# A transformer layer's tail in another order: one projection in the last attention step, a norm ahead of a gate, other work between products of one bank

## The chip, the cores and the metric

The kernel runs on one core of one Trainium2 chip. The metric is device microseconds (us) for one execution; a profile of one execution is read beside it. Engines: PE is TensorE (PEld are its weight loads), DVE is VectorE, ACT is ScalarE, POOL is GpSimd, SP is the engine that issues most transfers. PE writes its results into PSUM, which has eight banks, 0 to 7; DVE and ACT read them from there.

## The reference

```python
x = x + cross_attention(layernorm(x), ctx, ctx, mask)   # 16 heads of 16, 4096 keys, scores masked
x = x + retention(layernorm(x))                         # 4 heads, keys of 64, values of 128, rotary, decay, gated
x = x + experts(layernorm(x))                           # 8 dense experts, softmax gate, threshold 0.1

# retention(x): q, k, v, g = x Wq', x Wk', x Wv', x Wg';  q, k rotated
o = (q k' * decay) v;  o = o * rsqrt(mean(o * o) + eps) * gnorm_w
return (o * g * sigmoid(g)) Wo'
# experts(x): w = softmax(x Wgate + b); w[w < 0.1] = 0; w = w / sum(w)
return sum_e w[:, e] * (x W_e + b_e)
```

There are 2 batches of 256 queries with 256 features, so 512 rows of x: four tiles of 128 rows, t = 0 to 3. Tiles 0 and 1 are the first batch, tiles 2 and 3 the second.

## The kernel before, in words

Almost everything is float32 in SBUF, and every engine's program is one list written out by hand. Engines meet only through counting semaphores: `wait_ge(s, n)` holds an engine, and all that stands behind in its list, until the counter has reached n.

**The attention steps.** `steps` runs 56 steps (NU), seven blocks of 128 keys for each of eight stages (a stage is four heads of one batch). In step n PE computes the scores of step n (`scores`, L811) into banks 4 and 5, ACT takes their exponentials (`exps`, L1269), and PE multiplies those of step n-1 with the values (`weighted`, L826) into bank 6. Scores of the next step wait until ACT has read the bank. When a stage is complete, ACT copies the sums out (`outputs_out`, L1257), PE turns them into bank 7 (`turn_outputs`, L793), and DVE copies them into `acc` (`combine`, L1632). The last stage's copy, turn and combine stand at the very end of `steps`.

**Work of the first batch inside the steps.** The first batch's attention is complete long before step 46 (AT_TURNED). In step 46 PE turns its two tiles (`turn_at` 0 and 1, L878), in step 47 ACT takes them (`take_at`), in step 49 PE multiplies with the output weights (`attention_out` 0 and 1, L898), and in step 50 DVE, after `combine` of stage 6, adds the residual (`first_stream(0)`, L1663, needs `o_ready`) and computes the norm ahead of the retention (`layernorms`, L1485 to L1480). A norm is a chain of some dozen small DVE instructions in which each waits for the one before, and it ends with two wide ones (L1480) that write `xn`.

**The tail.** `tail_of_all` holds the rest. DVE first divides the second batch's attention by its sums (`attention_tokens(1)`, L1656), which needs the last `combine`. PE turns the normed tiles 0 and 1 (`turn_xn`), and per tile computes three projections of 512 columns each (`project_ret(t, m)`, L917): m = 0 is q and k into bank 2, m = 1 is v into bank 3, m = 2 is the gate into bank 4. Between those of tile 0 stand `turn_at(2)`, `turn_at(3)` and `attention_out` of 2 and 3. Each bank is single: `project_ret(t, m)` for t over 0 waits until the reader of tile t-1 is done, for bank 4 that is DVE's `gate_product` (L1697, needs ACT's tanh, L1320, and counts `gated_ready`). DVE's list for t = 0: the rotary products of bank 2 (L1678 to L1693), `first_stream(1)`, `gate_product(0)`, and then the second batch's norm.

Turned tiles go through banks 0 and 1, later bank 0 alone, in the fixed order TURNS; a turn waits for ACT's take of the turn before it (`turn_taken`). Outputs of the retention, gate logits and biases (SIDES) share bank 2 in the same manner: each waits until DVE has read the one before (`side_taken`).

Then follow, on PE: retention scores and values of the first batch, the last projections, and for the outputs `retention_out(t)` (L990, eight instructions into bank 2), read by DVE at L1736. The experts come in pairs: `pair(t, pr)` (L1010) multiplies a tile with two experts' weights in two halves over the input features (c = 0 and 1, weights in `ctxT` and `kpart`), into one of four banks (5, 6, 1, 7 in turn), and waits until DVE has read what stood there four pairs ago (`pair_read`). DVE adds each expert with its weight (`add_experts`, L1773), which needs the gate weights; those are computed for two tiles at a time (`gate_weights`, L1759 to L1765, last one writes `nwts`) and turned by PE (`turn_weights`) for the bias product (`biases`, L1021). Each tile is written out when its eight experts have been added.

Of the kernel before, what the change touches and what calls it, by code (L numbers as in the profile page):

```python
# [202 lines left out]
def build(nc, a):  # L203
    with ExitStack() as ctx:
# [437 lines left out]
        def _(pe):  # L642
# [188 lines left out]
            def steps(c):  # L831
                for n in range(NU):
# [29 lines left out]
                    if n == AT_TURNED + 3 and not c.loop:  # L862
                        attention_out(0)
                        attention_out(1)
                weighted(c, NU - 1)
                turn_outputs(c, STAGES - 1)
# [42 lines left out]

            def tail_of_all():  # L910
                def project_ret(t, m):

                    taken("n2", t)
                    if t:
                        pe.wait_ge(s[("rope_read", "v_taken", "gated_ready")[m]], t)
                    for c in range(KIN):
                        mm = pe.matmul(bank[:, 2 + m, :], xnT[:, c, t * P:(t + 1) * P], w_ret[:, c, m * 512:(m + 1) * 512],  # L917
                                       start=(c == 0), stop=(c == KIN - 1))
                    mm.then_inc(s["proj_ready"], 1)

# [4 lines left out]
                pe.wait_ge(s["late_loaded"], 16 * 10)  # L925
                turn_xn("n2", 0)
                turn_xn("n2", 1)
                for t in range(TT - 1):
                    project_ret(t, 0)
                    if t == 0:  # L930
                        turn_at(2)
                        turn_at(3)
                    if t:
                        turn_qk(t - 1)
                    project_ret(t, 1)
                    if t == 0:
                        attention_out(2)
                        attention_out(3)
                    if t:
                        turn_xn("n2", t + 1)  # L940
                    project_ret(t, 2)
# [62 lines left out]
                def pair(t, pr):  # L1004

                    m = t * (NE // 2) + pr
                    if m >= len(PAIR_BANKS):
                        pe.wait_ge(s["pair_read"], 2 * (m - len(PAIR_BANKS) + 1))
                    for c in range(KIN):
                        mm = pe.matmul(bank[:, PAIR_BANKS[m % 4], :], xnT[:, c, t * P:(t + 1) * P],  # L1010
                                       w_exp[c][:, 2 * pr:2 * pr + 2, :], start=(c == 0), stop=(c == KIN - 1))
                    mm.then_inc(s["pair_ready"], 1)
# [13 lines left out]
                retention_out(0)  # L1026
                retention_out(1)

                ret_values(RH)
# [17 lines left out]
                retention_out(2)  # L1047
                retention_out(3)
                turn_weights(1)
                pair(1, 0)  # L1050
# [9 lines left out]
                pair(2, 1)  # L1060
                turn_weights(2)
                pair(2, 2)
# [68 lines left out]
            with pe.If(fast < 1):  # L1131
# [25 lines left out]
                attention_out(1)  # L1157
                tail_of_all()

        @block.scalar  # L1160
        def _(act):
# [109 lines left out]
            def steps(c):  # L1271
                for n in range(NU):
# [11 lines left out]
                    if n == AT_TURNED + 1 and not c.loop:  # L1284
                        act.wait_ge(s["wo_loaded"], 32)
                        take_at(0)
                        take_at(1)
                outputs_out(c, STAGES - 1)
# [21 lines left out]
            def tail_of_all():  # L1310
# [33 lines left out]
                take_xn("n2", 0)  # L1344
                take_xn("n2", 1)
# [73 lines left out]
            with act.If(fast < 1):  # L1419
# [17 lines left out]
                take_at(1)  # L1437
                tail_of_all()
# [3 lines left out]
        def _(dve):  # L1442
# [191 lines left out]
            def steps(c):  # L1634
                for n in range(NU):
# [7 lines left out]
                    if n == AT_TURNED + 4 and not c.loop:  # L1643
# [23 lines left out]
            def tail_of_all():  # L1667
# [31 lines left out]
                for t in range(TT - 1):  # L1699
# [4 lines left out]
                    if t == 0:  # L1704
                        first_stream(1)
                    gate_product(t)
                    if t == 0:
                        layernorms("dve_post", x1, range(QT, TT), "n2_ready")
# [176 lines left out]
```

## Time and profile before

| what | value |
|---|---|
| median of three runs | 241.67 us |
| lowest, highest of them | 239.74, 241.96 us |
| the profiled execution's own time | 239.15 us |
| its span, first to last instruction | 237.2 us |
| PE, DVE, ACT busy, share of the span | 91%, 65%, 47% |
| mean granted TensorE clock | 0.995 |

Times in rows are us from the span's start. A row of the timeline gives start, duration, engine, line, operation, result <- operands, and in brackets how long the engine stood idle before and which instruction ended that. Ends of matmuls are modelled, and the next one can start a little before the row's end. "x4" merges four instructions that follow each other. A float32 matmul appears as two instructions.

### The profile page before, as it was taken

How to read it: one execution, taken by the hardware profiler on the slowest of the kernel's cores; microseconds unless marked ns; L12 is line 12 of the kernel's file. 1: busy time of each engine (PE TensorE's matmuls, PEld its weight loads, DVE VectorE, ACT ScalarE, POOL GpSimd, SP SyncE). 2: the span in 40 equal slices, each digit the busy share in tenths (PEclk: the TensorE clock that was granted, in tenths of full speed). 3: DMA queues.
4: the chain of work that ended last, by engine and by line, in shares of the span. 5: the costliest groups of instructions: out<-in, count | busy, mean ns of one | idle time of the engine just before them, and what ended most of it. 6: DMA issues, size and time to landing. Idle time of an engine off the chain costs nothing.

```text
span 237.2 us, 3690 instructions
## 1 busy us (share of the span) xinstructions
PE 215.2 (91%) x1314; PEld 115.7 (49%) x1314; DVE 154.4 (65%) x352; ACT 111.5 (47%) x238; POOL 36.6 (15%) x45
## 2 busy tenths in 40 slices
PE   8799997889799999999998989988988998899892
PEld 8367543344454544444443535445746754544340
DVE  6793888954928479787880346585184728585682
ACT  3227855575557487878889664233242051101000
POOL 8006998204503100000000000000000000000000
PEclk9999999999999999999999999999999999999998
DMA  5699673777099000920000000000000000000000
GB/s 182 216 228 322 191 199 94 190 185 260 14 237 221 4 1 3 284 73 3 3 3 1 0 3 1 0 0 0 3 0 0 0 4 1 0 0 22 23 26 26
DMA packets 15391, 17.93 MB, mean 76 GB/s; under 512 B 2600, under 2 KB 14472, under 8 KB 15368
## 3 DMA queue, kind: packets, MB, share of 16 engines
q1 hardware_dynamic: 14072, 17.30, 25.9%
q10 hardware_dynamic: 1296, 0.34, 0.8%
q8 instruction: 12, 0.20, 0.4%
q14 instruction: 11, 0.09, 0.1%
HBM read 9.79 MB, written 0.52 MB: 43 GB/s over the span
## 4 chain that ended last, share of the span: by engine, by line
PE 60%; DVE 16%; DMA 6%; ACT 5%; POOL 5%; issue 4%; SPq 3%; POOLq 0%; DVEq 0%; ACTq 0%
PE bank L826 10%; PE bank L811 10%; PE bank L1010 8%; PE bank L751 7%; PE bank L917 6%; DVE cneg L1592 4%; PE bank L990 3%; PE bank L878 3%; PE bank L711 3%; DMA ctxT<-in_ctxT 3%; DMA mask_all<-in_mask 2%; ACT prob L1269 2%; PE bank L698 2%; SPq L400 2%; PE bank L898 2%
## 5 line engine op out<-in xcount | busy, mean ns | idle before, releaser
L1592 DVE TENSOR_REDUCE cneg<-bank 128x1 f32<-128x896 f32 x64 | 68.1, 1087 | 24.2 <-PE bank L751 23.4
L1269 ACT ACTIVATE prob<-bank 128x512 f32<-128x512 f32 x112 | 65.6, 597 | 24.2 <-PE bank L811 21.7
L811 PE MATMUL bank<-qstack,kstack 100*128 100x256 bf16 x224 | 42.3, 274 | 3.4 <-ACT prob L1269 2.0
L751 PE MATMUL bank<-kstack,qstack 97*128 97x448 bf16 x128 | 34.7, 353 | 3.1 <-DVE cneg L1592 3.0
L826 PE MATMUL bank<-prob,vals 128*32 128x256 f32 x448 | 35.8, 391 | 0.4 <-ACT prob L1269 0.4
L811 PEld LDWEIGHTS bank<-qstack,kstack 100*128 100x128 bf16 x224 | 17.3, 97 | 31.6 <-ACT prob L1269 15.6
L917 PE MATMUL bank<-w_late,xnT 128*128 128x512 f32 x48 | 22.0, 595 | 0.3 <-ACT xnT L1298 0.3
L1010 PE MATMUL bank<-ctxT,xnT 128*128 128x512 f32 x32 | 17.1, 616 | 0.3 <-DVE x_in L1773 0.3
L1773 DVE SCALAR_TENSOR_TENSOR x_in<-bank,nwts,x_in 128x256 f32<-128x256 f32 x32 | 15.5, 484 | 2.5 <-PE bank L1010 1.4
L1010 PE MATMUL bank<-kpart,xnT 128*128 128x512 f32 x32 | 16.3, 592 | 0.0
L751 PEld LDWEIGHTS bank<-kstack,qstack 97*128 97x128 bf16 x128 | 11.5, 98 | 8.9 <-DVE cneg L1592 4.2
L826 PEld LDWEIGHTS bank<-prob,vals 128*32 128x32 f32 x448 | 8.8, 108 | 14.3 <-issue 11.2
L698 PE MATMUL bank<-ctxT,wk 128*128 128x448 f32 x32 | 13.3, 548 | 0.4 <-DMA ctxT<-in_ctxT 0.3
L711 PE MATMUL bank<-wv,ctxT 128*128 128x256 f32 x56 | 13.0, 381 | 0.1
L1632 DVE COPY acc<-bank 128x136 f32<-128x136 f32 x8 | 2.4, 299 | 15.7 <-PE bank L793 15.5
L917 PEld LDWEIGHTS bank<-w_late,xnT 128*128 128x128 f32 x48 | 8.5, 190 | 8.2 <-issue 7.7
L1298 ACT ACTIVATE xnT<-bank 128x256 f32<-128x256 f32 x8 | 3.0, 383 | 19.7 <-PE bank L878 19.7
L711 PEld LDWEIGHTS bank<-wv,ctxT 128*128 128x128 f32 x56 | 10.4, 190 | 2.1 <-DVE cneg L1592 0.4
L1010 PEld LDWEIGHTS bank<-kpart,xnT 128*128 128x128 f32 x32 | 6.1, 190 | 7.6 <-issue 7.6
L990 PE MATMUL bank<-w_late,kstack 128*128 128x256 f32 x32 | 7.7, 384 | 1.3 <-DVE mask_all L1736 1.3
L698 PEld LDWEIGHTS bank<-ctxT,wk 128*128 128x128 f32 x32 | 5.8, 190 | 5.3 <-issue 4.1
L1232 ACT COPY vals<-bank 128x512 f32<-128x512 f32 (+3 forms) x6 | 3.9, 658 | 8.7 <-PE bank L711 8.7
(151 smaller groups left out, 260.2 us busy)
## 6 DMA issues: line engine op xcount, KB each, us to landing
kstack<-kpart SPq DMA_DIRECT2D x24, 224.0 KB
w_late<-in_w_ret SPq DMA_DIRECT2D x1, 1536.0 KB
mask_all<-in_mask SPq DMA_DIRECT2D x2, 512.0 KB, 5.1
ctxT<-in_w_exp SPq DMA_DIRECT2D x1, 1024.0 KB
kpart<-in_w_exp SPq DMA_DIRECT2D x1, 1024.0 KB
ctxT<-in_ctxT SPq DMA_DIRECT2D x2, 448.0 KB, 5.5
ctxT<-in_ctxT SPq DMA_DIRECT2D x1, 896.0 KB, 7.4
qstack<-acc SPq DMA_DIRECT2D x12, 64.0 KB, 3.0
```

The costliest lines, as they stand in the source:

```text
L698: mm = pe.matmul(bank[:, c.key_banks(n) + h, 0:HC], wk[:, i, f * P:(f + 1) * P], ctxT[:, b, i, h * HC:(h + 1) * HC], start=(i == 0), stop= ...
L711: mm = pe.matmul(out[:, (k - blocks[0]) * D:(k - blocks[0] + 1) * D], ctxT[:, b, i, k * P:(k + 1) * P], wv[:, i, :], start=(i == 0), stop= ...
L751: mm = pe.matmul(out, qstack[0:MROW + 1, h, b, qt * P:(qt + 1) * P], kstack[0:MROW + 1, b, h, half_ * HC:(half_ + 1) * HC], start=True, st ...
L811: mm = pe.matmul(out[:, hh * NQ:(hh + 1) * NQ], kstack[0:KROWS, b, h, kt * P:(kt + 1) * P], qstack[0:KROWS, h, b, :], start=(hh == 0 or no ...
L826: mm = pe.matmul(bank[32 * j:32 * j + PADV, OB, 0:NQ], vals[:, b, kt, e:e + PADV], prob[:, (2 * u + j // 2) % PROBS, (j % 2) * NQ:(j % 2 + ...
L878: mm = pe.transpose(out[:, f * P:(f + 1) * P], src[:, f * width:(f + 1) * width], ident[:, :])
L917: mm = pe.matmul(bank[:, 2 + m, :], xnT[:, c, t * P:(t + 1) * P], w_ret[:, c, m * 512:(m + 1) * 512], start=(c == 0), stop=(c == KIN - 1))
L990: mm = pe.matmul(out[:, 0:D], yT[:, c, t * P:(t + 1) * P], w_reto[:, c, :], start=(c == 0), stop=(c == 3))
L1010: mm = pe.matmul(bank[:, PAIR_BANKS[m % 4], :], xnT[:, c, t * P:(t + 1) * P], w_exp[c][:, 2 * pr:2 * pr + 2, :], start=(c == 0), stop=(c = ...
L1269: act.activation(prob[:, n % PROBS, :], bank[:, S0 + jj, :], ACT.Exp).then_inc(c["prob_ready"], 1)
L1592: dve.tensor_reduce(cneg[:, st % 2, i:i + 1], bank[:, pair:pair + 2, 0:HC], AXXY, ALU.max, negate=True).then_inc(c["max_read"], 1)
L1773: dve.scalar_tensor_tensor(x_in[:, t, :], src, nwts[:, t, e:e + 1], x_in[:, t, :], ALU.mult, ALU.add).then_inc(s["pair_read"], 1)
```

## The change

It touches the order of instructions only; what is computed, and every buffer and bank, stays.

1. In the steps, `attention_out` of tiles 0 and 1 moves from step 49 to 48; DVE's `first_stream(0)` and the first batch's norm move from step 50 to 48, and so ahead of `combine` of stage 6.
2. The turns of the normed tiles 0 and 1 and ACT's takes of them move from the start of the tail to the end of the steps, ahead of the last `weighted` (PE) and ahead of the last `outputs_out` (ACT). `project_ret(0, 0)` moves ahead of the last `turn_outputs`.
3. DVE computes the second batch's norm before `gate_product(0)` and not after it.
4. `ret_values(RH)` moves between `retention_out(0)` and `retention_out(1)`.
5. `pair(1, 0)` is split: its first half goes between `retention_out(2)` and `retention_out(3)`, its second behind `turn_weights(1)` as before.
6. `pair(2, 2)` moves ahead of `turn_weights(2)`, so the two turns of weights stand next to each other.

```diff
@@ PE, steps
-                    if n == AT_TURNED + 3 and not c.loop:
+                    if n == AT_TURNED + 2 and not c.loop:
                         attention_out(0)
                         attention_out(1)
+                if not c.loop:
+                    turn_first_half()
                 weighted(c, NU - 1)
+                if not c.loop:
+                    project_ret(0, 0)
                 turn_outputs(c, STAGES - 1)
@@ PE, new function
+            def turn_first_half():
+
+                pe.wait_ge(s["late_loaded"], 16 * 10)
+                turn_xn("n2", 0)
+                turn_xn("n2", 1)
@@ PE, tail_of_all
-                pe.wait_ge(s["late_loaded"], 16 * 10)
-                turn_xn("n2", 0)
-                turn_xn("n2", 1)
                 for t in range(TT - 1):
-                    project_ret(t, 0)
+                    if t:
+                        project_ret(t, 0)
                     if t == 0:
                         turn_at(2)
                         turn_at(3)
...
-                def pair(t, pr):
+                def pair(t, pr, halves=(0, 1)):
 
                     m = t * (NE // 2) + pr
-                    if m >= len(PAIR_BANKS):
+                    if m >= len(PAIR_BANKS) and 0 in halves:
                         pe.wait_ge(s["pair_read"], 2 * (m - len(PAIR_BANKS) + 1))
-                    for c in range(KIN):
+                    for c in halves:
...
                 retention_out(0)
+                ret_values(RH)
                 retention_out(1)
 
-                ret_values(RH)
...
                 retention_out(2)
+                pair(1, 0, (0,))
                 retention_out(3)
                 turn_weights(1)
-                pair(1, 0)
+                pair(1, 0, (1,))
                 biases(1)
...
                 pair(2, 1)
+                pair(2, 2)
                 turn_weights(2)
-                pair(2, 2)
                 turn_weights(3)
                 biases(2)
@@ ACT, steps and tail_of_all
+                if not c.loop:
+                    take_xn("n2", 0)
+                    take_xn("n2", 1)
                 outputs_out(c, STAGES - 1)
...
-                take_xn("n2", 0)
-                take_xn("n2", 1)
@@ DVE, steps
-                    if n == AT_TURNED + 4 and not c.loop:
+                    if n == AT_TURNED + 2 and not c.loop:
                         first_stream(0)
                         layernorms("dve_post", x1, range(QT), "n2_ready")
@@ DVE, tail_of_all
                     if t == 0:
                         first_stream(1)
+                        layernorms("dve_post", x1, range(QT, TT), "n2_ready")
                     gate_product(t)
-                    if t == 0:
-                        layernorms("dve_post", x1, range(QT, TT), "n2_ready")
```

The branch for a mask that the fast path can't handle gets the same calls in the same order; it isn't taken with these inputs. Line numbers in the changed kernel are higher by 4 (L878 to L882, L898 to L902), 3 (L917 to L920), 8 (L990 to L998, L1010 to L1018), 10 (L1021 to L1031) and 16 (DVE's).

How instructions stand on PE at the end of the steps, before. L811 are scores, L826 `weighted`, L793 the last `turn_outputs`, L878 turns (of `xn`, the normed tiles, and of `vals`, the second batch's attention), L917 projections:

```order
L811 MATMUL bank<-qstack,kstack 128x256 x4
L826 MATMUL bank<-prob,vals 32x256 x8
L793 MATMUL bank<-ident,outT 128x128 x2
L878 MATMUL bank<-ident,xn 128x128 x4
L917 MATMUL bank<-w_late,xnT 128x512 x2
L878 MATMUL bank<-ident,vals 128x128 x4
L917 MATMUL bank<-w_late,xnT 128x512 x2
```

The same place on PE after the change:

```order
L811 MATMUL bank<-qstack,kstack 128x256 x4
L826 MATMUL bank<-prob,vals 32x256 x4
L882 MATMUL bank<-ident,xn 128x128 x4
L826 MATMUL bank<-prob,vals 32x256 x4
L920 MATMUL bank<-w_late,xnT 128x512 x2
L793 MATMUL bank<-ident,outT 128x128 x2
L882 MATMUL bank<-ident,vals 128x128 x4
L920 MATMUL bank<-w_late,xnT 128x512 x2
```

The four turns of `xn` have moved between the last two `weighted`, and the first projection has moved from behind the turn of `outT` to ahead of it; the turns of `vals` now follow that turn directly.

On DVE, in the tail for tile 0, before: L1690 and L1693 end the rotary work, L1663 is `first_stream(1)`, L1697 `gate_product(0)`, and from L1485 on it is the second batch's norm, of which the start is shown:

```order
L1690 TENSOR_TENSOR kstack<-kstack 128x8x32
L1693 TENSOR_TENSOR kstack<-kstack 128x8x32
L1663 TENSOR_TENSOR mask_all<-bank,xbo 128x256 x2
L1697 SCALAR_TENSOR_TENSOR kstack<-kstack,bank 128x512
L1485 BN_STATS stats<-mask_all 128x6 x2
L1473 BN_AGGR moments<-stats 128x2 x2
```

And on DVE after the change, the end of the same norm and what follows it (L1496 is the norm's last line, L1713 `gate_product`, L1694 to L1709 the rotary work of tile 1):

```order
L1482 TENSOR_TENSOR nw<-nw 128x2
L1483 SCALAR_TENSOR_TENSOR nw<-nw 128x2
L1496 TENSOR_SCALAR xn<-mask_all,moments,nw 128x256 x2
L1713 SCALAR_TENSOR_TENSOR kstack<-kstack,bank 128x512
L1694 TENSOR_TENSOR kstack<-bank,rope 128x512
L1695 TENSOR_TENSOR kstack<-bank,rope 128x512
```

The gate product now comes after the whole norm and right before the rotary products of tile 1.

On PE among the experts of tile 2, before: L1010 in twos is one pair, L878 of `nwts` a turn of gate weights, L1021 the bias product:

```order
L1010 MATMUL bank<-ctxT,xnT 128x512
L1010 MATMUL bank<-kpart,xnT 128x512
L878 MATMUL bank<-ident,nwts 8x128
L1010 MATMUL bank<-ctxT,xnT 128x512
L1010 MATMUL bank<-kpart,xnT 128x512
L878 MATMUL bank<-ident,nwts 8x128
L1021 MATMUL bank<-b_exp,wT 128x256
```

After:

```order
L1018 MATMUL bank<-ctxT,xnT 128x512
L1018 MATMUL bank<-kpart,xnT 128x512
L1018 MATMUL bank<-ctxT,xnT 128x512
L1018 MATMUL bank<-kpart,xnT 128x512
L882 MATMUL bank<-ident,nwts 8x128 x2
L1031 MATMUL bank<-b_exp,wT 128x256
```

Pair (2, 2) stands ahead of both turns of weights, and nothing stands between the two.

## Rows read from the trace of the kernel before

**Rows 1.** The page: busy us, share of the span, instructions of each engine.

```profile
PE 215.2 (91%) x1314; PEld 115.7 (49%) x1314; DVE 154.4 (65%) x352; ACT 111.5 (47%) x238; POOL 36.6 (15%) x45
```

**Rows 2.** Waits of PE: who <- for whom: us in total, times, longest.

```profile
PE bank L990 <- DVE mask_all L1736: 1.3, 2, 0.7
PE bank L878 <- DVE xn L1480: 1.2, 1, 1.2
```

**Rows 3.** Timeline of steps 47 to 50.

```profile
128.30 0.64 PE L826 MATMUL bank<-prob,vals 128*32 128x256 f32 x8
128.55 0.40 ACT L1298 ACTIVATE xnT<-bank,bv 128x128 f32<-128x128 f32 x1
...
130.87 2.00 PE L898 MATMUL bank<-wo,xnT 128*128 128x256 f32 x8
...
133.12 1.08 ACT L1269 ACTIVATE prob<-bank 128x512 f32<-128x512 f32 x2 [1.74 <-PE bank L811]
...
134.49 0.74 DVE L1663 TENSOR_TENSOR mask_all<-bank,xbo 128x256 f32<-128x256 f32 x2
```

**Rows 4.** Timeline of the last step and the start of the tail.

```profile
140.56 0.64 PE L826 MATMUL bank<-prob,vals 128*32 128x256 f32 x8 [0.39 <-ACT prob L1269]
141.26 0.37 ACT L1257 COPY outT<-bank 128x256 f32<-128x256 f32 x1 [0.76 <-PE bank L826]
141.69 0.44 PE L793 MATMUL bank<-ident,outT 128*128 128x128 f32 x2 [0.49 <-ACT outT L1257]
...
142.23 0.30 DVE L1632 COPY acc<-bank 128x136 f32<-128x136 f32 x1 [2.98 <-PE bank L793]
142.38 0.66 ACT L1298 ACTIVATE xnT<-bank 128x256 f32<-128x256 f32 x2 [0.74 <-PE bank L878]
...
142.81 1.98 PE L917 MATMUL bank<-w_late,xnT 128*128 128x512 f32 x4 [0.25 <-ACT xnT L1298]
142.95 0.76 DVE L1656 TENSOR_TENSOR vals<-acc,rsum 128x256 f32<-128x256 f32 x2
...
145.07 1.88 PE L917 MATMUL bank<-w_late,xnT 128*128 128x512 f32 x4
...
146.79 1.89 PE L898 MATMUL bank<-wo,xnT 128*128 128x256 f32 x8
```

**Rows 5.** Timeline of the second batch's residual, gate product and norm.

```profile
148.72 0.42 DVE L1663 TENSOR_TENSOR mask_all<-bank,xbo 128x256 f32<-128x256 f32 x1 [0.34 <-PE bank L898]
...
151.13 0.69 DVE L1697 SCALAR_TENSOR_TENSOR kstack<-kstack,bank 128x512 f32<-128x512 f32 x1 [1.99 <-ACT kstack L1320]
...
152.39 1.88 PE L917 MATMUL bank<-w_late,xnT 128*128 128x512 f32 x4
...
154.97 0.74 DVE L1480 TENSOR_SCALAR xn<-mask_all,moments,nw 128x256 f32<-128x256 f32 x2
155.44 0.44 PE L878 MATMUL bank<-ident,xn 128*128 128x128 f32 x2 [1.17 <-DVE xn L1480]
```

**Rows 6.** Timeline around the last gate weights.

```profile
217.77 1.00 DVE L1773 SCALAR_TENSOR_TENSOR x_in<-bank,nwts,x_in 128x256 f32<-128x256 f32 x2
...
220.25 0.27 PE L878 MATMUL bank<-ident,nwts 128*8 128x128 f32 x1 [0.99 <-DVE nwts L1765]
...
220.56 0.27 ACT L1298 ACTIVATE wT<-bank 8x128 f32<-8x128 f32 x1 [2.00 <-PE bank L878]
...
222.28 0.69 PE L1021 MATMUL bank<-b_exp,wT 8*128 8x256 f32 x2
```

**Rows 7.** Timeline: what PE waits for behind the two retention outputs.

```profile
188.30 0.56 DVE L1714 TENSOR_TENSOR kstack<-bank,decay 128x384 f32<-128x384 f32 x1
...
212.73 1.13 PE L1010 MATMUL bank<-ctxT,xnT 128*128 128x512 f32 x2 [0.31 <-DVE x_in L1773]
```

**Rows 8.** Stretches: length, PE, PEld, DVE, ACT, POOL busy; clock; DMA share, GB/s.

```profile
60.00:65.00 5.00, 3.59 (x31) 2.18 (x28) 4.73 (x6) 2.71 (x5) 2.50 (x2) 1.00 0.02 5
...
230.00:237.00 7.00, 2.58 (x7) 0.79 (x5) 2.19 (x5) 0.00 (x0) 0.00 (x0) 0.86 0.08 23
```

More of the change, by code:

```diff
@@ L907, in turn_xn, with project_ret @@
                 turn(kind, t, bank[:, turn_bank(kind, t), :], xn[:, t, :], KIN)
-            def tail_of_all():
[L911 to L915, printed above, removed]
-                    for c in range(KIN):
-                        mm = pe.matmul(bank[:, 2 + m, :], xnT[:, c, t * P:(t + 1) * P], w_ret[:, c, m * 512:(m + 1) * 512],
-                                       start=(c == 0), stop=(c == KIN - 1))
-                    mm.then_inc(s["proj_ready"], 1)
+            def project_ret(t, m):
+                taken("n2", t)
+                if t:
+                    pe.wait_ge(s[("rope_read", "v_taken", "gated_ready")[m]], t)
+                for c in range(KIN):
+                    mm = pe.matmul(bank[:, 2 + m, :], xnT[:, c, t * P:(t + 1) * P], w_ret[:, c, m * 512:(m + 1) * 512],
+                                   start=(c == 0), stop=(c == KIN - 1))
+                mm.then_inc(s["proj_ready"], 1)
+            def turn_first_half():
+                pe.wait_ge(s["late_loaded"], 16 * 10)
+                turn_xn("n2", 0)
+                turn_xn("n2", 1)
+            def tail_of_all():
                 def turn_qk(t):
@@ L923, in turn_qk @@
                     turn("qk", t, bank[:, TB, :], qk_rot[:, t % 2, :], 4)
-                pe.wait_ge(s["late_loaded"], 16 * 10)
-                turn_xn("n2", 0)
-                turn_xn("n2", 1)
                 for t in range(TT - 1):
-                    project_ret(t, 0)
+                    if t:
+                        project_ret(t, 0)
                     if t == 0:
@@ L1002, in logits @@
                     mm.then_inc(s["side_ready"], 1)
-                def pair(t, pr):
+                def pair(t, pr, halves=(0, 1)):
                     m = t * (NE // 2) + pr
-                    if m >= len(PAIR_BANKS):
+                    if m >= len(PAIR_BANKS) and 0 in halves:
                         pe.wait_ge(s["pair_read"], 2 * (m - len(PAIR_BANKS) + 1))
-                    for c in range(KIN):
+                    for c in halves:
                         mm = pe.matmul(bank[:, PAIR_BANKS[m % 4], :], xnT[:, c, t * P:(t + 1) * P],
-                                       w_exp[c][:, 2 * pr:2 * pr + 2, :], start=(c == 0), stop=(c == KIN - 1))
-                    mm.then_inc(s["pair_ready"], 1)
+                                       w_exp[c][:, 2 * pr:2 * pr + 2, :], start=(c == 0), stop=(c == KIN - 1),
+                                       skip_group_check=True)
+                    if KIN - 1 in halves:
+                        mm.then_inc(s["pair_ready"], 1)
                 def turn_weights(t):
@@ L1157, in _ @@
                 attention_out(1)
+                turn_first_half()
+                project_ret(0, 0)
                 tail_of_all()
@@ L1437, in _ @@
                 take_at(1)
+                take_xn("n2", 0)
+                take_xn("n2", 1)
                 tail_of_all()
```

## The prediction

> **What bounds the kernel now.** I read the page first. PE is busy for 91% of the span, DVE for 65% [rows 1], so what the order of the work can win is PE's idle time, and only where PE's own list is what ends last. Then I read PE's waits in the tail, after 138 us. Three are 1 us or more in total: for the reader of bank 2 between retention outputs (1.3 us in two waits) and for DVE's norm result `xn` (1.2 us, one wait) [rows 2], and for the last gate weights `nwts` (0.99 us, one wait) [rows 6]. Each edit from number 3 on aims at one of them. Last came the timeline, to see what ends each wait and what else stands in the way once it is gone.
>
> The steps are a loop between PE (scores) and ACT (exponentials); a PE instruction that has nothing to do with it lengthens a step when ACT runs dry. In step 49 that happens: `attention_out` holds PE for 2.00 us from 130.87, and ACT stands idle for 1.74 us before its next exponentials at 133.12 [rows 3].
>
> **Edits 1: output product and first norm in step 48.** Before, PE has issued `weighted` of step 47 at 128.30 and could go on at about 128.9; ACT's take of tile 1 ends at 128.55 + 0.40 = 128.95 [rows 3]. So `attention_out` (two times some 0.95 us) now runs from 128.9 to 130.8, in time in which PE partly waited for ACT. The two exponentials of step 49 follow: scores out at 130.8, and from PE's scores to ACT's start I take 0.4 us, so ACT begins at 131.2, needs 1.08 us for two [rows 3] and 0.37 for the copy of stage 6 [rows 4], and can start step 50 at about 132.7 instead of 133.12. That is 0.4 us won. The bounds: nothing, if the product only moves the wait by one step; 0.6 us if no part of it shows up again. I take 0.4. DVE starts the residual at about 130 and the norm at 131.4 rather than at 135.2; a norm takes 155.71 - 151.82 = 3.9 us [rows 5], so it is done at 135.4. `combine` of stage 6 waits behind it until 135.4; its bank 7 is next wanted by the last `turn_outputs` after 141 us [rows 4], six us later, so this costs nothing.
>
> **Edits 2: turns, takes and one projection in the last step.** All times here are those of before less the 0.4. The four turns of `xn` (0.43 us) fill PE's 0.39 us idle ahead of the last `weighted` [rows 4], so that stays at 140.15. ACT takes the two tiles in 0.66 us [rows 4], 140.1 to 140.8, and is free when the last `weighted` ends at 140.8: no cost to the copy of `outT`. PE then starts `project_ret(0, 0)` at 140.7, not 142.81 [rows 4]. Four instructions of 512 columns keep PE for 1.72 us (145.07 to 146.79, with nothing between [rows 4]), to 142.4. But the last `turn_outputs` stood at 141.69 and now stands behind them, at 142.4. What hangs on it: DVE's `combine` 0.54 us later, the reciprocal, and the two halves of the second batch's attention, done at about 143.37 and 143.71 before [rows 4], that is 1.7 and 2.0 us behind the turn. Now they are done at 144.1 and 144.45. PE's next instructions are exactly the turns of these tiles, so PE stands idle from 142.7 to 144.15: a wait of about 1.4 us that was not there. `project_ret(0, 1)` starts at about 144.75 against 145.07 [rows 4]. So the pair of edits 1 and 2 is worth 0.3 us, of which the first gave 0.4: moving the projection trades a filled gap for a new one and loses 0.1. Its bounds: had the turn not been delayed, 145.07 - 143.8 = 1.3 us would be won; were another 0.5 us lost on the way from `combine`, 0.4 is lost in place of 0.1.
>
> **Edit 3: the norm before the gate product.** Before, DVE has the residual at 149.14, stands idle for 1.99 us for tanh, does the gate product (151.13, 0.69 us), then the norm; `xn` of tile 2 arrives at 155.38 and PE starts its turn at 155.44 after 1.17 us idle [rows 5]. PE's queue was in fact free 1.72 us after 152.39, at 154.11, so the wait costs 1.33 us. After, the norm runs from 149.15 to 153.1 and the gate product to 153.8 (in times of before; both shift by the 0.3). `xn` is there at 152.8, ahead of PE at 154.1: the wait is gone. What is late next: `project_ret(1, 2)` writes bank 4 and so needs the gate product; PE gets to it at 154.4, 0.6 us after it is done. The rotary products of tile 1, queued behind the norm on DVE before as well, start at 153.9 instead of 155.75. So nothing follows that takes the gain back, and all 1.33 us pass through. Bounds: 1.17 (the row's idle time) and 1.33; I take 1.3.
>
> **Edits 4 and 5: nothing.** `ret_values(RH)` is three products of 128 columns, six instructions, some 0.65 us at the projections' 1.72 us for four times 512, and fills one of the two waits of [rows 2] (0.6 us). But the second `retention_out` can't start earlier, since it waits for DVE in either order. From its result DVE runs residual, norm and, inside the norm, two decay products; PE's last retention values wait for the one at 188.30 to 188.86 [rows 7], and the turn of `xn` after them for the end of the norm. The chain is DVE's, PE only waits later: 0. In the same way half of `pair(1, 0)` (0.86 us, half of four times 512 columns) fits into the other wait (0.7 us, plus the 0.16 by which a modelled end overlaps the next start, 145.07 + 1.88 - 146.79 [rows 4]), and PE has 0.86 us less to do behind; but pair (1, 3) waits at 212.73 for an expert that DVE adds inside and behind the third norm [rows 7], and the norm starts when `retention_out(3)` has ended. 0 again. Bounds for the two together: 0.2 us lost, where the filler is longer than the gap, and 1.1 us won, if PE and not DVE were last in both places; the rows say DVE, so I take 0.
>
> **Edit 6: pair (2, 2) ahead of both turns of weights.** Before, PE waits 0.99 us for `nwts` and turns at 220.25 [rows 6]; with the 0.16 its queue is free from 219.1. Pair (2, 2) needs the bank that expert 5 of tile 1 leaves at 218.77 [rows 6], before PE is there: no new wait. It fills 219.1 to 220.8, by when the weights (220.19) are there. Then come two turns in a row, and the second must wait for ACT's take of the first: 220.56 + 0.27 - 220.25 = 0.58 us after its start [rows 6] plus some 0.1 to come back, where nothing was waited for before and the turn itself took 0.2. So 0.5 us go back and 0.6 are won. From there PE has work without a gap to its end (biases, 0.69 us, then five pairs of 1.72 us), and DVE's last two experts follow the last pair: the gain reaches the end. Bounds: 0.3 if the take comes later, 1.1 if it costs nothing; I take 0.6.
>
> **Sum.** 0.4 - 0.1 + 1.3 + 0 + 0.6 = 2.2 us. Against the profiled execution: 239.15 - 2.2 = 236.95 us. The median of the runs is 241.67, 2.5 us above it, and the runs spread over 2.2 us; the time I forecast is 241.67 - 2.2 = 239.5 us, 0.9% below.
>
> **Rivals.**
> Rival A, the tail waits give more. If PE's list ends last at the places of edits 4 and 5, they add up to 1.1 us: 3.3 us, 238.4. For it: the waits of 1.3 us are real [rows 2]. Against: what follows them waits for DVE [rows 7].
> Rival B, a wait takes the place of another. The new 1.4 us wait for the attention tiles is longer (its chain is combine, reciprocal, product, turn over two engines), and edit 6's second turn waits for more than its 0.5: then edit 3 alone stays, 1.3 us, 240.4. For it: in both places the change itself makes the waiting instruction come sooner behind what it needs. Against: each link has its row.
> Rival C, the clock. The new idle stretch of PE before the turns, right behind the idle in the steps, lets the granted TensorE clock fall from 2.4 to 1.2 GHz, and the projections that follow run at half speed. Each us of PE's work at half clock costs one us; past 2.2 us of it the change is slower than before, and if it lasts for the 5 us of work from 144.2 on, the sum is -2.2 + 5 = +2.8: 244.5. For it: the granted clock did fall once, to 0.86 over the stretch from 230 to 237 us, after PE's last matmul had ended [rows 8]. Against: in 60 to 65 us PE was idle for 1.4 of 5 us and the clock stayed at 1.00 [rows 8].
> The Trainium skill ("TensorE: Matmul & The Clock Gate", Part 1) states that the gate halves the clock of an array that has been idle and gives it back only after sustained work. By that rule a reordering that gathers PE's idle time in one place can lose more than it moves; the stretch at 60 us does not show it for idle time of this size.
>
> **Chances.** Forecast (1.8 to 2.6 us won) 0.55; A or anything above 2.6 us 0.17; B 0.20; C 0.05; others 0.03. A measurement of this kernel tells about 1%, 2.4 us, from no change, and the forecast of 0.9% lies just inside, so its share is split by the noise: 0.29 faster, 0.26 within. With A's 0.17 that makes faster by over 1% 0.46; B, the rest and half of the others give within 1% 0.48; slower by over 1% is C and a rest, 0.06. The range: down to A and a low draw of the runs (the profiled 239.15 less 2.2 is 236.95) 236.8; up to B with the upper run of the spread, 241.3.
>
> **What would show it right or wrong.** In the profile of the changed kernel: ACT's idle time before step 50's exponentials falls from 1.74 us, and they start 0.4 us earlier; PE has a wait of about 1.4 us for the turns of the attention tiles; PE's 1.17 us wait for `xn` is gone and the first turn of tile 2 comes 1.6 us earlier than 155.44; the wait for bank 2 in front of `retention_out` is gone, but the distance from that output to the third norm and to pair (1, 3) is the same; between the two last turns of weights lie 0.6 us in which PE waits for ACT, and the bias product comes 2.2 us earlier than 222.28. Wrong it would be if the granted clock shows anything below 1.00 after 142 us, if `project_ret(1, 2)` waits for the gate product, or if the span from 156 us to the end shrinks by more than edit 6's 0.6 us.

## The result, and the profile after

The changed kernel takes 237.39 us (median of 4 runs, 237.17 to 239.12) against 240.83 (4 runs, 239.74 to 241.96): ratio 0.9887, 95% interval 0.9842 to 0.9932. Timed again later in 12 runs it gave 0.9914 (0.9875 to 0.9952). The forecast was 2.2 us, 0.9% less; the two measurements say 1.1% and 0.9%. In microseconds the forecast was 239.5. The profiled execution took 237.40 us with a span of 235.5, against 239.15 and 237.2.

The page's first rows of the changed kernel (busy us, share of the span, instructions), to be held against [rows 1]:

```profile
PE 215.2 (91%) x1314; PEld 115.7 (49%) x1314; DVE 154.5 (66%) x352; ACT 111.4 (47%) x238; POOL 36.7 (16%) x45
```

The work is the same to 0.1 us on each engine; only idle time went. PE's waits in the whole span of the changed kernel (who <- for whom: us, times, longest), against [rows 2]:

```profile
PE bank L977 <- DVE kstack L1729: 1.6, 2, 0.9
...
PE bank L882 <- DVE vals L1672: 1.2, 1, 1.2
...
PE bank L1018 <- DVE x_in L1788: 0.7, 2, 0.4
...
PE bank L882 <- ACT wT L1314: 0.4, 1, 0.4
```

All three waits the edits aimed at are gone from the list (bank 2's reader 1.3 us, `xn` 1.2, `nwts` 1.0). Four have grown or appeared: 1.2 us for the second batch's attention tiles (L882 <- L1672), which is edit 2's; the wait for the decay products (L977, from 1.0 to 1.6 us), which is what edit 4's filler ran into; that for an expert sum (L1018, from 0.3 to 0.7), edit 5's; and 0.4 us for ACT's take of the turned weights (L882 <- wT L1314), edit 6's.

Since executions differ ahead of the `weighted` of step 47, whichever kernel runs (it starts at 128.30 us in the profile before, at 128.74 after, and at up to 130.8 in those below), the comparison goes by four distances, all from start to start of rows of the timeline:
- S1: from the `weighted` of step 47, which PE runs in step 48, to `project_ret(0, 1)`
- S2: from there to the three projections of tile 3
- S3: from there to `pair(1, 3)`
- S4: from there to DVE's last two expert sums.

| us | S1 | S2 | S3 | S4 | sum |
|---|---|---|---|---|---|
| before | 16.77 | 25.32 | 42.34 | 19.96 | 104.39 |
| after | 16.37 | 23.93 | 42.35 | 19.41 | 102.06 |
| edit that changes it | 1 and 2 | 3 | 4 and 5 | 6 | |
| forecast of the difference | -0.3 | -1.3 | 0 | -0.6 | -2.2 |
| measured | -0.40 | -1.39 | +0.01 | -0.55 | -2.33 |

The two profiled executions themselves lie only 1.75 us apart, since the changed kernel's reached step 47 0.44 us later and took 0.19 us more behind its last expert sums (4.70 in place of 4.51). Both are stretches that the change doesn't touch.

The timeline of steps 48 to 50 on ACT, after, against [rows 3]:

```profile
129.25 1.12 ACT L1282 ACTIVATE prob<-bank 128x512 f32<-128x512 f32 x2
131.56 1.08 ACT L1282 ACTIVATE prob<-bank 128x512 f32<-128x512 f32 x2 [1.19 <-PE bank L811]
132.53 0.38 ACT L1270 COPY outT<-bank 128x256 f32<-128x256 f32 x1
```

ACT's idle time is 1.19 us instead of 1.74, one step earlier. The end of the steps, after, against [rows 4]:

```profile
139.90 0.66 PE L882 MATMUL bank<-ident,xn 128*128 128x128 f32 x4
...
140.48 0.64 PE L826 MATMUL bank<-prob,vals 128*32 128x256 f32 x8
...
141.05 1.98 PE L920 MATMUL bank<-w_late,xnT 128*128 128x512 f32 x4
...
142.87 0.38 PE L793 MATMUL bank<-ident,outT 128*128 128x128 f32 x2
143.29 0.30 DVE L1648 COPY acc<-bank 128x136 f32<-128x136 f32 x1 [7.18 <-PE bank L793]
...
144.01 0.76 DVE L1672 TENSOR_TENSOR vals<-acc,rsum 128x256 f32<-128x256 f32 x2
144.49 0.78 PE L882 MATMUL bank<-ident,vals 128*128 128x128 f32 x4 [1.24 <-DVE vals L1672]
...
145.11 1.88 PE L920 MATMUL bank<-w_late,xnT 128*128 128x512 f32 x4
```

The turn of `outT` starts 2.39 us behind the last `weighted` (142.87 - 140.48) where it was 1.13 (141.69 - 140.56), and PE stands idle for 1.24 us right after it. Next, edit 3's place, after, against [rows 5]:

```profile
148.75 0.42 DVE L1679 TENSOR_TENSOR mask_all<-bank,xbo 128x256 f32<-128x256 f32 x1 [0.34 <-PE bank L902]
...
152.42 1.88 PE L920 MATMUL bank<-w_late,xnT 128*128 128x512 f32 x4
152.46 0.73 DVE L1496 TENSOR_SCALAR xn<-mask_all,moments,nw 128x256 f32<-128x256 f32 x2
...
153.23 0.69 DVE L1713 SCALAR_TENSOR_TENSOR kstack<-kstack,bank 128x512 f32<-128x512 f32 x1
...
154.14 0.38 PE L882 MATMUL bank<-ident,xn 128*128 128x128 f32 x2
```

The turn of tile 2 has no bracket any more: it starts 1.72 us behind 152.42, when the queue lets it, and not when `xn` is there (it was, at 153.2). And edit 6's place, after, against [rows 6]:

```profile
219.47 0.27 PE L882 MATMUL bank<-ident,nwts 128*8 128x128 f32 x1
219.78 0.27 ACT L1314 ACTIVATE wT<-bank 8x128 f32<-8x128 f32 x1 [2.56 <-PE bank L882]
220.19 0.27 PE L882 MATMUL bank<-ident,nwts 128*8 128x128 f32 x1 [0.45 <-ACT wT L1314]
220.39 0.69 PE L1031 MATMUL bank<-b_exp,wT 8*128 8x256 f32 x2
```

The wait for `nwts` is gone, and the second turn now waits 0.45 us for ACT's take of the first.

### The profile page after: what moved, and what is told of

Its sections match the earlier page's. It is cut to its first block, busy times and chain, and to the rows that moved or that the text cites. A ratio compares the mean times of both kernels' runs of the same rounds, so it can differ in the third digit from the quotient of the medians.

```text
span 235.5 us, 3689 instructions
## 1 busy us (share of the span) xinstructions
PE 215.2 (91%) x1314; PEld 115.7 (49%) x1314; DVE 154.5 (66%) x352; ACT 111.4 (47%) x238; POOL 36.7 (16%) x45
## 4 chain that ended last, share of the span: by engine, by line
PE 62%; DVE 15%; DMA 6%; POOL 5%; ACT 4%; issue 3%; SPq 3%; POOLq 0%; ACTq 0%; DVEq 0%
PE bank L826 11%; PE bank L811 10%; PE bank L1018 8%; PE bank L920 7%; PE bank L751 7%; DVE cneg L1608 4%; PE bank L882 3%; PE bank L998 3%; DMA ctxT<-in_ctxT 3%; PE bank L711 3%; DMA mask_all<-in_mask 2%; ACT prob L1282 2%; PE bank L698 2%; SPq L400 2%; PE bank L902 2%
## 5 line engine op out<-in xcount | busy, mean ns | idle before, releaser
L811 PE MATMUL bank<-qstack,kstack 100*128 100x256 bf16 x224 | 42.3, 274 | 3.1 <-ACT prob L1282 1.4
L826 PE MATMUL bank<-prob,vals 128*32 128x256 f32 x448 | 35.8, 391 | 0.0
L811 PEld LDWEIGHTS bank<-qstack,kstack 100*128 100x128 bf16 x224 | 17.4, 97 | 31.1 <-ACT prob L1282 16.0
L920 PE MATMUL bank<-w_late,xnT 128*128 128x512 f32 x48 | 22.0, 595 | 0.0
L1018 PE MATMUL bank<-ctxT,xnT 128*128 128x512 f32 x32 | 17.2, 619 | 0.7 <-DVE x_in L1788 0.7
L1018 PE MATMUL bank<-kpart,xnT 128*128 128x512 f32 x32 | 16.3, 592 | 0.0
L826 PEld LDWEIGHTS bank<-prob,vals 128*32 128x32 f32 x448 | 8.8, 108 | 13.6 <-issue 11.0
L920 PEld LDWEIGHTS bank<-w_late,xnT 128*128 128x128 f32 x48 | 8.6, 190 | 8.1 <-issue 7.7
L1314 ACT ACTIVATE xnT<-bank 128x256 f32<-128x256 f32 x8 | 3.0, 385 | 18.0 <-PE bank L882 17.9
L1018 PEld LDWEIGHTS bank<-kpart,xnT 128*128 128x128 f32 x32 | 6.0, 190 | 7.3 <-issue 7.2
L1018 PEld LDWEIGHTS bank<-ctxT,xnT 128*128 128x128 f32 x32 | 5.2, 190 | 5.6 <-DVE x_in L1788 3.3
```

The costliest lines, as they stand in the source:

```text
L811: mm = pe.matmul(out[:, hh * NQ:(hh + 1) * NQ], kstack[0:KROWS, b, h, kt * P:(kt + 1) * P], qstack[0:KROWS, h, b, :], start=(hh == 0 or no ...
L826: mm = pe.matmul(bank[32 * j:32 * j + PADV, OB, 0:NQ], vals[:, b, kt, e:e + PADV], prob[:, (2 * u + j // 2) % PROBS, (j % 2) * NQ:(j % 2 + ...
```

## The experiments

Each is compared by the four distances; its time is a ratio to the kernel before, timed on the same chip in the same rounds. There are only one or two profiles of each kernel, so how well a distance repeats matters: where two kernels have the same order in a distance and the granted clock stays up, their profiles agree in it to 0.02 us (S2 is 25.32 or 25.33 without edit 3 and 23.93 or 23.94 with it; S3 is 42.34 to 42.36 everywhere).

### Edit 3 alone

```diff
+                        layernorms("dve_post", x1, range(QT, TT), "n2_ready")
                     gate_product(t)
-                    if t == 0:
-                        layernorms("dve_post", x1, range(QT, TT), "n2_ready")
```

> The kernel before with edit 3 alone (second batch's norm ahead of the first gate product). Landmarks on PE: from the start of project_ret(0,1) to the start of tile 3's projections 25.32 us before, 23.93 with the whole change. Theory (the wait for xn was all that edit 3 had to remove, nothing late behind it): 24.0 us, 1.3 us less in all, and the wait of 1.17 us of PE for xn is gone; everything else as before. Rival (the gain needs the other edits, or project_ret(1,2) now waits for the gate product): 24.6 to 25.3 us, with a wait of PE for the gate product.

Measured: S2 23.93 us; S1, S3 and S4 as before (16.79, 42.34, 19.95). Ratio 0.9948 (0.9901 to 0.9996). In its timeline the turn of tile 2 follows the projection 1.72 us after it, with no wait:

```profile
154.92 1.88 PE L917 MATMUL bank<-w_late,xnT 128*128 128x512 f32 x4
156.64 0.38 PE L878 MATMUL bank<-ident,xn 128*128 128x128 f32 x2
```

Edit 3 gives its 1.39 us (25.32 - 23.93) by itself and needs nothing of the others.

### Edit 1 alone

```diff
-                    if n == AT_TURNED + 3 and not c.loop:
+                    if n == AT_TURNED + 2 and not c.loop:
                         attention_out(0)
...
-                    if n == AT_TURNED + 4 and not c.loop:
+                    if n == AT_TURNED + 2 and not c.loop:
                         first_stream(0)
```

> The kernel before with edit 1 alone (attention_out and first norm in step 48). From the start of weighted in step 47 to the start of project_ret(0,1): 16.77 us before, 16.37 with edits 1 and 2. Theory (edit 1 is worth 0.65 us, more than the 0.4 forecast, and edit 2 gives 0.25 of it back): 16.1 us. Rival (edit 1 is worth 0.4 as forecast and edit 2 costs nothing): 16.4 us.

Measured: S1 16.12 us, 0.65 less; the rest as before. Ratio 0.9954 (0.9916 to 0.9992). ACT's rows of its steps 49 to 51:

```profile
131.21 1.08 ACT L1269 ACTIVATE prob<-bank 128x512 f32<-128x512 f32 x2 [1.19 <-PE bank L811]
132.18 0.38 ACT L1257 COPY outT<-bank 128x256 f32<-128x256 f32 x1
132.43 1.12 ACT L1269 ACTIVATE prob<-bank 128x512 f32<-128x512 f32 x2
```

From the first exponential of step 49 to that of step 50 pass 1.22 us (132.43 - 131.21). I had added the rows' durations, 1.08 + 0.37 = 1.45; but the rows of ACT overlap, the next starts before the end of the one before.

### Edit 6 alone

```diff
                 pair(2, 1)
+                pair(2, 2)
                 turn_weights(2)
-                pair(2, 2)
                 turn_weights(3)
```

> The kernel before with edit 6 alone (pair (2,2) ahead of both turns of weights). From the start of pair (1,3) to DVE's last two expert sums: 19.96 us before, 19.41 with the whole change. Theory: 19.4 us, with a wait of some 0.45 us for ACT between the two turns. Rival (the rest of edit 5 is needed for it, or DVE is last): 19.7 to 20.0.

Measured: S4 19.41 us, the rest as before. The time doesn't show it (ratio 0.9976, 0.9934 to 1.0018): 0.55 us are a quarter of a per cent. The distance is what says it.

### Edit 2 alone

```diff
+                if not c.loop:
+                    turn_first_half()
                 weighted(c, NU - 1)
+                if not c.loop:
+                    project_ret(0, 0)
                 turn_outputs(c, STAGES - 1)
```

(with ACT's takes of `xn` ahead of its last `outputs_out`.)

> The kernel before with edit 2 alone (turns of xn and project_ret(0,0) in the last step). From weighted of step 47 to project_ret(0,1): 16.77 us before. Theory (edit 2 is a loss of 0.25 us): 17.0 us, slower than before by 0.2 to 0.3. Rival (edit 2 costs 0.1 or gains): 16.6 to 16.9 us.

Measured: S1 17.09 us, 0.32 more than before; S2 and S4 as before; ratio 1.0018 (0.9985 to 1.0051). By the distance edit 2 is a loss; the time alone doesn't tell it from no change. S3 was 44.02 in its profile, 1.68 more than before. That this isn't the edit is seen in the changed kernel, which has it too and an S3 of 42.35: the granted clock was lower here, and that is taken up below.

### The changed kernel with the projection back behind the turn

```diff
                 weighted(c, NU - 1)
-                if not c.loop:
-                    project_ret(0, 0)
                 turn_outputs(c, STAGES - 1)
+                if not c.loop:
+                    project_ret(0, 0)
```

> The changed kernel with project_ret(0,0) moved back behind the last turn_outputs; the early turns and takes of xn stay. Theory (the projection ahead of the turn delays combine and the attention tiles, and PE's new wait of 1.24 us is its price): the last turn starts 1.25 us sooner, PE waits 0.5 us for outT in place of 1.24 for the attention tiles, and the distance from weighted of step 47 to project_ret(0,1) is 15.2 to 15.4 us instead of 16.37, all of which reaches the end: 1.1 us less than the changed kernel. Rival (the chain from the last weighted over combine sets the time in either order, a wait is only moved): 16.2 to 16.4 us and no difference.

Measured: S1 15.30 us, 1.07 less than the changed kernel; S2 23.94, S3 42.36, S4 19.40. Ratio 0.9844 (0.9747 to 0.9942, 4 runs). PE's rows at the end of its steps:

```profile
142.35 0.64 PE L826 MATMUL bank<-prob,vals 128*32 128x256 f32 x8
143.48 0.44 PE L793 MATMUL bank<-ident,outT 128*128 128x128 f32 x2 [0.49 <-ACT outT L1270]
143.76 1.88 PE L920 MATMUL bank<-w_late,xnT 128*128 128x512 f32 x4
145.48 0.60 PE L882 MATMUL bank<-ident,vals 128*128 128x128 f32 x4
```

The turn of `outT` waits 0.49 us for ACT's copy, but then the projection covers DVE's chain to the attention tiles, and their turns come without a bracket. So the projection ahead of the turn filled a gap of 0.5 us and opened one of 1.24. The early turns of `xn` are the good half of edit 2: S1 is 15.30 here and 16.12 with edit 1 alone, 0.82 us less.

### The changed kernel with edits 4 and 5 undone

```diff
                 retention_out(0)
-                ret_values(RH)
                 retention_out(1)
+                ret_values(RH)
...
                 retention_out(2)
-                pair(1, 0, (0,))
                 retention_out(3)
                 turn_weights(1)
-                pair(1, 0, (1,))
+                pair(1, 0)
```

> The changed kernel with edits 4 and 5 undone (ret_values(RH) and pair (1,0) whole again). From the start of tile 3's projections to the start of pair (1,3): 42.34 us before, 42.35 with the change. Theory (DVE's chain is last there, the fillers are worth nothing): 42.3 to 42.4, PE waits for bank 2 again (0.6 and 0.7 us) and less for the decay product and xn behind. Rival (they fill real gaps): 42.9 to 43.5.

Measured: S3 42.35 us, and the sum of the four 102.05 against 102.06. Ratio 0.9916 (0.9878 to 0.9954). Its PE rows around the retention outputs:

```profile
182.25 1.97 PE L998 MATMUL bank<-w_late,kstack 128*128 128x256 f32 x8 [0.61 <-DVE mask_all L1750]
...
187.67 0.46 PE L977 MATMUL bank<-kstack 128*128 128x128 f32 x2 [0.23 <-DVE kstack L1728]
...
203.88 1.97 PE L998 MATMUL bank<-w_late,kstack 128*128 128x256 f32 x8 [0.68 <-DVE mask_all L1750]
```

and the same two places of the changed kernel:

```profile
181.18 1.97 PE L998 MATMUL bank<-w_late,kstack 128*128 128x256 f32 x8
...
186.61 0.46 PE L977 MATMUL bank<-kstack 128*128 128x128 f32 x2 [0.90 <-DVE kstack L1729]
...
202.83 1.95 PE L998 MATMUL bank<-w_late,kstack 128*128 128x256 f32 x8
```

From the second output to the retention values are 5.42 us in one and 5.43 in the other: the filler takes the 0.61 us wait away, and 0.67 us come back as a longer wait for the decay product (0.23 to 0.90). In edit 5's place the filler takes the 0.68 us wait away, and from that output to pair (1, 3) pass 8.56 us with the filler (211.39 - 202.83) and 8.57 without (212.45 - 203.88), since there too PE waits for what DVE computes behind the output:

```profile
208.60 1.13 PE L1018 MATMUL bank<-ctxT,xnT 128*128 128x512 f32 x2 [0.31 <-DVE x_in L1788]
...
211.39 1.12 PE L1018 MATMUL bank<-ctxT,xnT 128*128 128x512 f32 x2 [0.41 <-DVE x_in L1788]
```

These two rows are the changed kernel's. Without the filler only the second of the two waits is there, with 0.30 us.

### The projection back, and pair (2, 2) in halves

```diff
                 pair(2, 1)
-                pair(2, 2)
+                pair(2, 2, (0,))
                 turn_weights(2)
+                pair(2, 2, (1,))
                 turn_weights(3)
```

(and the projection behind the turn, as above.)

> The changed kernel with the projection back behind the turn, and pair (2,2) in two halves, the first ahead of turn_weights(2), the second between the two turns. Theory: as with the projection back alone, and the second turn of weights no longer waits 0.45 us for ACT: from pair (1,3) to DVE's last two sums 19.2 us in place of 19.41 (some 0.2 go to a wait for the weights), some 1.3 us less than the changed kernel in all. Rival (the wait for the weights takes all of it back): 19.4 us.

Measured: 15.30, 23.94, 42.36 and S4 19.09 us, a sum of 100.69, which is 3.70 less than before and 1.37 less than the changed kernel. Ratio 0.9829 (0.9776 to 0.9881, 6 runs). PE's rows between the turns:

```profile
218.30 0.27 PE L882 MATMUL bank<-ident,nwts 128*8 128x128 f32 x1
218.41 1.02 PE L1018 MATMUL bank<-kpart,xnT 128*128 128x512 f32 x2
219.27 0.27 PE L882 MATMUL bank<-ident,nwts 128*8 128x128 f32 x1
```

The half pair hides ACT's take; S4 is 0.32 us shorter, where I had expected 0.2. Timed again:

> The kernel of e7 (projection back behind the turn, pair (2,2) in halves) timed again. Theory: distances as in e7 (15.30, 23.94, 42.36, 19.09 us), 3.7 us less than the kernel before where the clock stays up, a ratio of 0.984 to 0.986 with the interval clear of 1. Rival (e7's ratio of 0.983 was a lucky draw of undisturbed clocks): 0.988 or higher.

It gave 0.9833 (0.9783 to 0.9884, 6 runs). Its distances came again too, 15.31, 23.93, 42.35 and 19.09 us. By the distances this version is the fastest of all that ran. By time it isn't told apart: its intervals and that of the changed kernel's longer timing (0.9875 to 0.9952) still overlap a little, and the interval of the kernel with only the projection put back (0.9747 to 0.9942) covers both.

### The wait for the attention tiles made longer

Rival C was that idle time of PE in front of the tail lowers the granted clock. Here DVE does work that nobody needs, so that PE waits longer at the same place: it repeats the reciprocal of the attention sums, and nothing is left out.

```diff
             def tail_of_all():
+                for _ in range(6):
+                    post(dve.reciprocal(rsum[:, NG:2 * NG, :], acc[:, NG:2 * NG, :, DK]))
                 attention_tokens(1)
```

> The changed kernel with six more reciprocals of the same tile on DVE ahead of attention_tokens(1), each waiting for the one before, some 0.37 us apiece: PE's wait for the attention tiles grows from 1.24 us to about 3.4. Theory (idle time of this size in one place does not by itself lower the granted clock): from weighted of step 47 to project_ret(0,1) 18.5 us in place of 16.37, and from there to tile 3's projections 23.9 as before, granted clock 1.00 behind the wait. Rival (the clock case of the prediction): the granted clock behind the wait falls to half, and the second distance grows by 1 to 2 us.

> The same with twelve: PE's wait about 5.5 us. Theory: first distance 20.7 us, second 23.9 at clock 1.00. Rival (clock): the second distance is 1.7 us or more longer, as in the projection-alone run a stretch at half clock made a distance 1.7 us longer; the mean clock of all its runs lies lower than that of the changed kernel.

Measured with six: S1 18.98 us and S2 24.98, 1.05 more than in the changed kernel. Ratio 1.0090 (1.0047 to 1.0133), though the changed kernel's 0.9887 to 0.9914 with 2.3 us (0.0096) of added waiting would have made 0.998 to 1.001. PE's rows:

```profile
143.38 0.38 PE L793 MATMUL bank<-ident,outT 128*128 128x128 f32 x2
147.33 1.11 PE L882 MATMUL bank<-ident,vals 128*128 128x128 f32 x4 [3.56 <-DVE vals L1672]
```

and the stretches of it around the wait (columns as in [rows 8]: length; PE, PEld, DVE, ACT, POOL busy; granted clock; DMA):

```profile
144.00:147.00 3.00, 0.00 (x0) 0.00 (x0) 2.72 (x9) 0.00 (x0) 0.00 (x0) 0.98 0.00 0
147.00:150.00 3.00, 2.67 (x7) 1.59 (x8) 2.66 (x6) 1.14 (x4) 0.00 (x0) 0.50 0.00 0
150.00:153.00 3.00, 3.00 (x12) 2.18 (x11) 0.51 (x2) 0.58 (x1) 0.00 (x0) 0.95 0.00 0
```

The clock fell at the end of the wait to 0.50, the lower of its two levels (1.2 GHz), stayed there while PE worked from 147 to 150, and came back soon after. The four turns take 1.11 us in place of 0.78, and the projection behind them starts 0.90 us after their start (148.23 - 147.33) in place of 0.62. So S1 grew by 2.61 us, of which 2.32 are the longer wait and 0.29 are slower work. With twelve reciprocals PE waited 5.89 us, S1 was 21.30 and S2 25.12; ratio 1.0156 (1.009 to 1.0222, 4 runs). In neither kernel did any run have a mean clock over 0.992. The price of the clock beside the wait is the rest of S1 and the growth of S2: 0.29 + 1.05 = 1.34 us with six and 0.28 + 1.19 = 1.47 with twelve. My theory for these two is wrong, the clock case is right, for waits of this size. In the changed kernel, with its 1.24 us, the stretch behind the wait is not disturbed:

```profile
142.00:146.00 4.00, 2.76 (x12) 1.36 (x11) 2.60 (x6) 1.03 (x4) 0.00 (x0) 1.00 0.00 2
146.00:150.00 4.00, 4.00 (x15) 2.60 (x14) 2.46 (x7) 0.70 (x2) 0.00 (x0) 1.00 0.00 0
```

Nor did the clock fall behind this wait in the three other profiles that have it (1.2 to 1.3 us: edit 2 alone, edits 4 and 5 undone, the changed kernel again).

The Trainium skill ("TensorE: Matmul & The Clock Gate", Part 1) says that an idle array is gated down to half its clock; here that holds for the waits of 3.56 and 5.89 us, and was not seen behind one of 1.24. Between 1.3 and 3.56 us no run says where it begins.

### The changed kernel again

> The changed kernel as it is, timed again in more rounds. Theory: its runs at a mean granted clock of 0.995 and over lie at 237.0 to 237.6 us and those of the kernel before at 239.2 to 239.8, 2.2 us apart; runs with a lower mean clock are slower by some 2 us for each 0.01, in either kernel. Rival (the change also lowers or raises how often the clock dips): the shares of runs under 0.995 differ clearly between the two.

Measured, 12 runs: 238.90 us median (236.82 to 240.45), ratio 0.9914 (0.9875 to 0.9952); S1 to S4 16.36, 23.93, 42.34, 19.41. Its four runs with a mean clock of 0.995 and over took 236.82 to 237.52 us, mean 237.2; nine of the 23 runs of the kernel before did so too, 239.11 to 240.52, mean 239.8. That is 2.6 us apart, where this profile's distances give 2.35 and I had expected 2.2; the kernel before spread wider than I had said. With the first four runs 7 of 16 runs of the changed kernel had such a clock and 9 of those 23 of the one before: no clear difference.

## Why the prediction was right, point by point

**Edits 3 and 6 carry it, as forecast.** 1.39 and 0.55 us for 1.3 and 0.6, each shown by a kernel with that edit alone. What was to be late next also came out: the gate product is done at 153.9, before the projection that needs its bank, and the second turn of weights waits for ACT's take (0.45 us in the bracket, 0.5 forecast).

**Edit 1 was under-sized: 0.65 us, not 0.4.** The place and the mechanism are right, ACT's idle time fell from 1.74 to 1.19. The term that failed is ACT's time from one step to the next, for which I summed two rows (1.45 us) that overlap (1.22 measured); another 0.08 us are that step 49's exponentials start 2.82 us behind the `weighted` (131.56 - 128.74) and not 2.90. Step 50's exponentials gain 0.77 us (128.30 to 133.12 is 4.82 before, 128.74 to 132.79 is 4.05 after), of which 0.12 are lost again behind them.

**Edit 2 was under-sized too, as a loss: 0.25 us behind edit 1 and 0.32 alone, not 0.1.** The new wait for the attention tiles was forecast at 1.4 us and is 1.24. What I had put at nothing is the cover of the four turns of `xn`: with them the last `weighted` starts 11.74 us behind that of step 47 (140.48 - 128.74), without them 11.61 (edit 1 alone), so they don't quite fit into the 0.39 us gap. For the turn not being delayed I had given a bound of 1.3 us for edits 1 and 2 together; the kernel with the projection back got 1.47, above it by less than what edit 1 gave more. That the two edits together came so near the forecast (0.40 for 0.3) is in part luck: edit 1 was 0.25 us better and edit 2 0.15 us worse than forecast.

**Edits 4 and 5 at nothing** holds to 0.01 us, and for the reason given: DVE's chain of residual, norm and decay products ends last. The prediction counted three waits of 1 us or more in the tail; the one for the decay products, 1.0 us before, was a fourth, and it is the one into which edit 4's wait moved.

**The rivals.** A (the fillers pay) fell with edits 4 and 5 undone. B (edit 3 alone stays) fell with S1 and S4. C (the clock) didn't happen in the profile of the changed kernel, but it is no mere thought: the two kernels with a longer wait show it at this very place, with a price of 1.34 and 1.47 us beside the wait itself. My reason against it, the stretch at 60 us, was too weak to exclude it, as the next section shows.

**The sum** of 2.2 us agrees with 2.33 by the distances. That the first timing gave 3.4 us between the medians and 1.1% in ratio need not be a larger gain: four runs are few, three of the changed kernel's had a mean clock of 0.996 or more, and the longer timing gave 0.9%. The forecast in microseconds, 239.5, was the median of three runs, 241.67, less 2.2; the measured 237.39 is 2.1 us below it, nearly as much as the change is worth. So the time says little of the mechanism here, and the distances say it.

## What to carry to other kernels

Before filling a gap, ask who starts later because of the filler: a projection of 1.72 us put into a gap of 0.5, ahead of the instruction that starts a chain over two engines, cost a wait of 1.24 us behind it, and moving it back won 1.07. A wait of the busiest engine is worth removing only where its own list ends last; if another engine's chain follows from the same result, the wait reappears further on; here it did so to 0.01 us. And in sums of steps take the distance from start to start, not the durations of rows, which overlap.

## What the runs showed of the hardware that I had not expected

Much of the spread of this kernel's runs goes with TensorE's clock. In the 23 runs of the kernel before that were timed beside the two kernels with a longer wait, those with a mean granted clock of 0.995 to 1.000 took 239.1 to 240.5 us, those with 0.990 mostly 240.5 to 241.5, those with 0.983 or 0.984 242.2 to 242.9: some 2 us for each 0.01. One run, at 0.945, took 243.27 us and doesn't fit this. Nor is it all of the spread: runs at 0.995 and over are still 1.4 us apart, and PE's waits for the transfers into `ctxT`, ahead of step 47, add up to 0.2 to 2.7 us in the thirteen profiles. In that of the kernel with edits 4 and 5 undone, where the granted clock is 1.00 in every stretch ahead of step 47, they are 2.1 us, and its `weighted` of step 47 starts at 129.81 us in place of 128.30:

```profile
PE bank L698 <- DMA ctxT<-in_ctxT: 2.1, 3, 1.1
```

One dip of the clock is in the profile of edit 2 alone:

```profile
180.00:190.00 10.00, 9.31 (x42) 7.55 (x41) 4.27 (x15) 1.22 (x2) 0.00 (x0) 0.83 0.00 0
```

S3 was 1.68 us longer there, and the retention output of eight instructions (L998) took 3.20 us in place of 1.89. Another is in the kernel with the projection back, right behind the stretch that [rows 8] gave as a reason against rival C. In its profile PE was busy for 2.59 of 4 us, and then:

```profile
60.00:64.00 4.00, 2.59 (x26) 0.92 (x24) 3.93 (x7) 1.73 (x3) 3.20 (x3) 1.00 0.04 14
64.00:68.00 4.00, 4.00 (x15) 2.98 (x14) 1.68 (x2) 1.61 (x4) 0.00 (x0) 0.57 0.40 115
```

In the profiles of the kernels before and after the same stretch passed at 1.00. Six of the thirteen profiles have such a dip outside the two lengthened waits: this one, the same place in the timed-again kernel with the half pair (0.61 over 64 to 68 us), at 8 to 12 us with edit 3 alone (0.57), around 40 us in two others, and the one at 180. So one and the same list of instructions gets a dip at a place in one execution and none in another; what decides it, and whether fewer waits ahead of 64 us would make it rarer, wasn't tried and stays open.
